# Cross-attention and product-key experts on one core: the experts' first tile begins in four chunks of two heads

## The reference, cut to what matters

```python
x = x + attention(layernorm(x), ctx)
xn = layernorm(x)
q = xn @ w_q                                   # 512 -> 2048 = 16 parts of 128
q = (q - mean(q)) * rsqrt(var(q) + eps) * gamma + beta   # mean, var over all tokens
sim = einsum("pbnhd,hkpd->pbnhk", q, keys)     # 8 heads x 2 sides x 128 scores
sx, ix = top_k(sim[0], 8);  sy, iy = top_k(sim[1], 8)
scores, pk = top_k(sx[:, None] + sy[None, :], 8)         # 8 of 64 sums
indices = ix * 128 + iy at pk                  # 8 heads x 8 = 64 experts a token
h = gelu(x . down_embed[indices]) * softmax(scores)
x = x + sum_k h[k] * up_embed[indices[k]]
```

## Time and profile before

| | us |
|---|---|
| median of 3 runs (lowest to highest) | 3229.04 (3228.68 to 3231.35) |
| the profiled execution, whole | 3229.33 |
| its span in the trace | 3227.2 |
| busy in the span: PE / DVE / ACT / POOL | 2857.5 / 2407.8 / 1820.0 / 2141.3 |
| experts begin (first DVE instruction of the block) | 468.9 |
| first gather issued | 532.85 |
| last gather issued | 3186.17 |

### The profile page before, as it was taken

The page is one execution under the profiler, slowest core; times in us unless marked ns, Lnnn a source line. Parts: engine busy times, 40 slices in busy tenths (PEclk is TensorE's granted clock), DMA queues, the critical chain, the costliest instruction groups (busy, mean ns, idle before and its releaser), DMA issues.

```text
span 3227.2 us, 36087 instructions
## 1 busy us (share of the span) xinstructions
PE 2857.5 (89%) x10310; PEld 1373.1 (43%) x10310; DVE 2407.8 (75%) x5220; ACT 1820.0 (56%) x5589; POOL 2141.3 (66%) x2224
## 2 busy tenths in 40 slices
PE   8999999898888888888888888889888888888877
PEld 6777767343333333333333333333333333333322
DVE  5888715887777777777777777777777777777765
ACT  3566502665565555655656555555656555655554
POOL 1555513777777777777777777777777777777773
PEclk9999999999999999999999999999999999999999
DMA  6222103999999999999999999999999999999996
GB/s 226 80 70 75 39 30 141 395 412 411 413 412 411 412 412 412 411 412 412 412 411 413 412 412 412 412 411 411 412 409 408 411 411 410 411 408 406 409 410 246
DMA packets 324861, 1133.07 MB, mean 351 GB/s; under 512 B 36331, under 2 KB 36971, under 8 KB 324024
## 3 DMA queue, kind: packets, MB, share of 16 engines
q0 software_dynamic: 294912, 1073.87, 83.1%
q1 hardware_dynamic: 29088, 56.41, 4.9%
q10 hardware_dynamic: 664, 0.50, 0.1%
HBM read 1113.87 MB, written 16.78 MB: 350 GB/s over the span
## 4 chain that ended last, share of the span: by engine, by line
DMA 40%; PE 16%; POOL 14%; issue 11%; DVE 4%; ACT 0%; POOLq 0%; ACTq 0%; DVEq 0%
DMA rows<-in_table,expert_idx 37%; POOL rows L785 13%; PE banks L1330 11%; PE banks L1309 3%; DMA expert_more_rows<-in_table,expert_idx 3%; POOL expert_more_rows L785 1%; PE banks L1244 1%; DVE expert_top_i L889 1%; DVE expert_diag L980 1%; DVE rows L966 0%; PE banks L1256 0%; DVE expert_top_s L881 0%; DVE expert_coef L972 0%; PE banks L1285 0%; DVE expert_best_i L912 0%
## 5 line engine op out<-in xcount | busy, mean ns | idle before, releaser
L785 POOL DMA_INDIRECT rows<-in_table,expert_idx x1824 | 1725.1, 946 | 658.0 <-issue 541.0
L1330 PE MATMUL banks<-rows,expert_diag 128*128 128x512 f32 x3648 | 1710.9, 614 | 307.3 <-DVE expert_diag L980 307.0
L1149 ACT ACTIVATE rows<-rows 128x512 f32<-128x512 f32 x1824 | 1124.3, 617 | 945.2 <-DVE expert_coef L972 942.8
L966 DVE TENSOR_TENSOR rows<-rows,banks 128x2048 f32<-128x2048 f32 x456 | 1043.0, 2287 | 543.0 <-DMA rows<-in_table,expert_idx 541.5
L1330 PEld LDWEIGHTS banks<-rows,expert_diag 128*128 128x128 f32 x3648 | 687.4, 194 | 1283.0 <-issue 752.8
L1309 PE MATMUL banks<-amat,expert_xnT 128*128 128x512 f32 x992 | 465.2, 592 | 2.0 <-ACT banks L1140 1.3
L980 DVE TENSOR_TENSOR expert_diag<-banks,expert_coef 128x512 f32<-128x512 f32 x512 | 348.2, 680 | 0.6
L1149 ACT ACTIVATION_READ_ACCUMULATOR rows<-rows 128x1 f32 x1824 | 339.9, 186 | 0.0
L1309 PEld LDWEIGHTS banks<-amat,expert_xnT 128*128 128x128 f32 x992 | 188.3, 190 | 238.8 <-issue 229.9
L785 POOL DMA_INDIRECT expert_more_rows<-in_table,expert_idx x224 | 212.7, 950 | 84.1 <-issue 73.9
L1330 PE MATMUL banks<-expert_more_rows,expert_diag 128*128 128x512 f32 x448 | 209.8, 612 | 39.1 <-DVE expert_diag L980 39.1
(11 more groups left out here) (125 smaller groups left out, 2087.8 us busy)
## 6 DMA issues: line engine op xcount, KB each, us to landing
rows<-in_table,expert_idx POOLq DMA_INDIRECT x1824, 14.6
attention_xT_t<-in_x_T SPq DMA_DIRECT2D x32, 256.0 KB, 3.1
attention_x_t<-in_x SPq DMA_DIRECT2D x32, 256.0 KB, 3.1
x_dram<-rows SPq DMA_DIRECT2D x32, 256.0 KB, 2.0
expert_x_t<-x_dram SPq DMA_DIRECT2D x32, 256.0 KB, 6.1
out_y<-expert_x_t SPq DMA_DIRECT2D x32, 256.0 KB, 6.1
rows<-in_w_q SPq DMA_DIRECT2D x4, 1024.0 KB, 6.1
rows<-in_w_qT SPq DMA_DIRECT2D x4, 1024.0 KB, 8.6
```

Source lines behind the costliest of these rows:

```text
L785: pool.indirect_dma_start(four(n)[:, k, :], None, table[:, :], bass.IndirectOffsetOnAxis(ap=idx[:, t % 2, at:at + 1], axis=0))\
L966: return dve.tensor_tensor(down, down, xn_ps[:, par, :].unsqueeze(1).to_broadcast([P, HALF, D]), ALU.mult)
L1149: ins = act.activation(down, down, ACT.Copy, accum_out=hid[:, j % RING, k:k + 1])
L1330: mm = pe.matmul(out_ps[:, par, :], diag[:, j % RING, k, :], four(t * HALVES + j)[:, k, D:2 * D], start=(j == 0 and k == 0), stop=(j == HA ...
```

## The change

Nothing is different in what is computed, only how and in which order.

1. The query means move forward: the mean-token product is issued after 6 of the last 25 tiles of second moments (before: after 24), ACT keeps it (`mu_kept`), and DVE computes all 16 means and their squares at the end of the attention block (`query_means`).
2. The experts' start is done by quarters. PE interleaves C w for part m, the matrix of a quarter and tile 0's scores from that matrix; `raw_queries`, `norm_queries`, `first_scores` are gone. DVE scales the keys and spreads the offset for a quarter in one instruction each (in `fold`); `keys_scaled` and `offset_wide` lie now in the ring of x2 tiles, so SP's load of tile 2 waits for the matrix.
3. `choose_two(q)` decodes the indices of two heads, and POOL starts the gathers of 4 steps after each of four index events. Chunks 2 and 3 are chosen inside tile 0's steps 1 and 3.
4. Two of POOL's powers stand inside its gather list (ahead of steps 3 and 4); step 4 waits for the last C w, steps 6 and 8 for the matrix.
5. The scores and choices for tile 1 and 2 that stood ahead of the loop are now beside tile 0's steps (`first_tile`, and `beside_first` of ACT and PE). Exponentials of tile 0 are taken for two heads at a time.

```diff
+            def query_means():
+                dve.wait_ge(ev["mu_kept"], 1)
+                dve.wait_ge(w_in, 32 * KC)
+                for m in range(NM):
+                    wait(dve, "mean_done", m - 1)
+                    dve.tensor_tensor_reduce(free[:, m % 2 * D:(m % 2 + 1) * D], mu_row, wq2T[:, m, :],
+                                             1.0, 0.0, ALU.mult, ALU.add, mean_q[:, m:m + 1])\
+                       .then_inc(ev["mean_done"], 1)
...
-            second_moments(len(moments_left) - 1)
+            second_moments(6)
...
-            pe.matmul(out_ps, inv_tokens, xsum, start=True, stop=True)
-            second_moments(1)
+            pe.matmul(out_ps, inv_tokens, xsum, start=True, stop=True).then_inc(ev["mu_done"], 1)
+            second_moments(len(moments_left))
...
+            deviations(0)
+            deviations(1)
             for n in range(NT * HALVES):
                 t, j = divmod(n, HALVES)
-                if j % (HALVES // 2) == 0:
-                    wait(pool, "idx_done", t * 2 + j // (HALVES // 2) + 1)
+                if n in (3, 4):
+                    deviations(n - 1)
+                if t == 0 and j % 4 == 0:
+                    pool.wait_ge(ev["idx_done"], j // 4 + 1)
+                if t > 0 and j % (HALVES // 2) == 0:
+                    pool.wait_ge(ev["idx_done"], NQ + (t - 1) * 2 + j // (HALVES // 2) + 1)
                 if n >= GROUPS:
-                    wait(pool, "up_done", n + 1 - GROUPS)
-                if n == 6:
-                    wait(pool, "amat_done", NM)
+                    pool.wait_ge(ev["up_done"], n + 1 - GROUPS)
+                if n == 4:
+                    pool.wait_ge(ev["yw_done"], NM)
+                if n in (6, 8):
+                    pool.wait_ge(ev["a_done"], NM)
+                    pool.wait_ge(ev["bias_done"], NQ)
...
+            def first_tile():
+                for j in range(HALVES):
+                    dve.wait_ge(row_in[j % GROUPS], (j // GROUPS + 1) * 64)
+                    made_products = products(0, 0, j)
+                    if j == 0:
+                        made_products.then_inc(ev["multiplied"], 1)
+                        fold(NQ - 1)
+                        weigh_two(0)
+                        weigh_two(1)
+                        dve.wait_ge(ev["ident_kept"], 1)
+                    else:
+                        coefficients(0, 0, j - 1)
+                        diagonals(0, j - 1)
+                    if j == 1:
+                        choose_two(2, ())
+                    if j == 3:
+                        choose_two(3, ())
...
+            def beside_first(j):          # PE
+                if j == 8:
+                    turn(2)
+                early = {4: (1, 0), 5: (1, 1), 8: (1, 2), 9: (1, 3), 10: (2, 0), 12: (2, 1), 13: (2, 2),
+                         14: (2, 3)}
+                if j in early:
+                    scores(*early[j])
```

More of the change, by code:

```diff
@@ L715, in ring @@
         return (half % 2) * 2 + par
-    def run(step):
-        for t in range(NT):
-            step(t, t % 2, t // 2, min(3, NT - 1 - t), t == 0)
     with nc.Block() as block:
@@ L989, in finish, with step @@
                 dve.tensor_tensor(x2, out_ps[:, par, :], x2, ALU.add).then_inc(ev["y_done"], 1)
-            def step(t, par, half, more, first):
+            def step(t, par, half, more):
                 for j in range(HALVES):
@@ L994, in step @@
                     dve.wait_ge(row_in[n % GROUPS], (n // GROUPS + 1) * 64)
-                    made_products = products(t, par, j)
-                    if first and j == 0:
-                        made_products.then_inc(ev["multiplied"], 1)
+                    products(t, par, j)
                     if j in (4, 6, 11, 14) and more >= 2:
@@ L1009, in step @@
                             split_places(0)
-                        if not first:
+                        if t > 1:
                             indices(par, 1)
@@ L1023, in step @@
                             keep_marked(0)
-                        if not first:
-                            finish(t - 1, 1 - par, half + par - 1)
+                        finish(t - 1, 1 - par, half + par - 1)
                     if j == 6:
@@ L1069, in step @@
                         diagonals(t, j - 1)
-                    elif not first:
+                    else:
                         diagonals(t - 1, HALVES - 1)
@@ L1104, in _ @@
                 now(pick_marked())
-                indices(0, d)
-            shift_best().then_inc(ev["shifted"], 1)
-            norm(1, 1, 0)
-            wait(dve, "normed", NM)
-            wait(dve, "raw_done", NQ)
-            now(norm_again(0, 0, 0))
-            wait(dve, "exp_done", 1)
-            now(exp_sum())
-            now(exp_inverse())
-            now(weights(0))
-            top(1, 0)
-            top(1, 1)
-            wait(dve, "topped", NQ + 2)
-            now(pair_sums(0))
@@ new lines, in _ @@
+            dve.wait_ge(ev["consts"], 1)
+            now(dve.tensor_copy(iota_f[:, :], iota_u[:, :]))
+            keep_moments(1)
+            keep_moments(2)
+            query_variance(0)
+            norm(0, 0, 0)
+            for m in range(1, 4):
+                query_variance(m)
+            norm_again(0, 0, 0)
+            query_variance(4)
+            fold(0)
+            query_variance(5)
+            query_variance(6)
+            choose_two(0, (7,))
+            query_variance(8)
@@ L1127, in _ @@
+            fold(1)
+            norm(1, 1, 0)
+            query_variance(9)
+            query_variance(10)
+            choose_two(1, (11,))
+            query_variance(12)
+            query_variance(13)
+            fold(2)
+            query_variance(14)
+            query_variance(15)
+            first_tile()
+            for t in range(1, NT):
+                step(t, t % 2, t // 2, min(3, NT - 1 - t))
             coefficients(NT - 1, 1, HALVES - 1)
@@ L1169, in step, with early_seed, exponents_of_two @@
                         turned(t + 3, 1 - par)
-                    if j == 7 and more >= 1:
+                    if t > 0 and j == 7 and more >= 1:
                         exponents()
+            def beside_first(j):
+                if j == 0:
+                    turned(1, 1)
+                if j == 1:
+                    exponents_of_two(2)
+                if j == 3:
+                    exponents_of_two(3)
+                    early_seed(1, 0)
+                if j == 4:
+                    early_seed(1, 1)
+                if j == 6:
+                    early_seed(1, 2)
+                if j == 7:
+                    early_seed(1, 3)
+                if j == 8:
+                    turned(2, 0)
+                if j == 9:
+                    early_seed(2, 0)
+                if j == 10:
+                    early_seed(2, 1)
+                if j == 12:
+                    act.wait_ge(ev["shifted"], NQ + 1)
+                    exponents().then_inc(ev["exp_done"], 1)
+                    early_seed(2, 2)
+                if j == 13:
+                    early_seed(2, 3)
+            def early_seed(t, q):
+                wait(act, "topped", t * NQ + q - 1)
+                seed(q)
+            def exponents_of_two(q):
+                two = slice(2 * q, 2 * q + 2)
+                act.wait_ge(ev["shifted"], q + 1)
+                act.activation(expo[:, two, :], expo[:, two, :], ACT.Exp).then_inc(ev["exp_done"], 1)
             def keep_moments(j):
@@ L1313, in score, with scores, step @@
                     mm.then_inc(ev["scored"], 1)
-            def step(t, par, half, more, first):
+            def scores(t, q):
+                for c in range(KC):
+                    score(t, t % 2, q, c)
+            def step(t, par, half, more):
                 chunk_at = {0: 0, 2: 1, 8: 2, 11: 3}
```

420 lines of the change are left out of this document (227 added, 193 removed).

## The result

| | us | runs |
|---|---|---|
| before | 3229.82 (3228.68 to 3231.61) | 7 |
| after | 3239.47 (3237.34 to 3240.72) | 7 |
| after / before | 1.0028, 95% interval 1.0017 to 1.0040 | |

The changed kernel is slower by 0.28%, some 9.7 us, where I had forecast 3221 and faster. The time lies above my range of 3214.5 to 3228. The profiled execution of after took 3239.55 us (its span 3237.8), 10.2 us more than the one of before.

What follows compares the result with a forecast made beforehand. DMA, full at 411 GB/s, bounds the main loop. From 3229.33 us, 10.7 us of earlier landing off and 2.15 us of clock loss on give 3220.8; 0.29 lower for the median, 3220.5, said as 3221; range 3214.5 to 3228.

Steps and rivals of the forecast that it cites:

- means: Means moved from the experts' variance loop to the attention block: 12 us of DVE, hidden there, so 0 us.
- nothing is won there by itself: Experts' variance loop: PE sets its pace at 2.16 us a part, so removing DVE's mean reductions alone gains nothing.
- the start: Before tile 0's loop: first gather at about 503.4, 29.4 us earlier; DVE at step 1 at 537.1.
- tile 0 gives most of it back: Tile 0's steps: slots wait for updates, DVE leaves at 641.1, 97th gather at 649.3; 10.7 us of advance left.
- the clock takes one loss: Tile 0's early updates: PE's waits lower its granted clock, one loss of 2.15 us on the path.
- The landing that I compare: Landing of the 97th gather (step 24, after tile 0's last update): 655.8 against 666.5, 10.7 us earlier.
- the two waits: PE before tile 0's loop: 2.1 us for scaled keys and 1.5 us for variances, matrix done at about 535.9.
- the 10 us of waits in my sum of 104.0: DVE in tile 0: waits for PE's scores of tiles 1 and 2, which stand behind an update, 10 us.
- tables: ACT's exponential and gelu switches in tile 0: 1.28 us load each on the path, without 1.38 us drain each.
- So the DMA stays full and the 10.7 us are kept to the end.: From tile 1 on: unchanged code, a step of four gathers takes 5.18 us at 411 GB/s, nothing of the advance lost.
- The rivals: Tile 0 takes back more, 0.30; slower, 0.08; advance holds or half, 0.06; start not earlier, 3229 or above.
- the one that ended slower: PE stays at 1.2 GHz until tile 0's step 7: 3248, or about 3233 for half the steps; chance 0.08.

Runs made afterwards that it cites:

- Experiment 11: Changed kernel with more_rows realigned to 512 bytes, and the 16 means and squares back in the experts' variance loop: 3225.07 us, ratio 0.9982 to the kernel before.
- experiment 12: Changed kernel with rows and more_rows at multiples of 512 bytes, PE's scores of tiles 1 and 2 one step earlier: 3164.78 us, 0.9796 to before.
- a_aligned: Changed kernel with 448 unused bytes ahead of more_rows, which then lies at a multiple of 512: 3222.57 us, ratio 0.9975 to the kernel before.
- Experiments 1 to 6: Unused padding tiles: one realigns more_rows in the changed kernel (3222.57 us), five shift more_rows or the tiles behind it in the kernel before (3231.91 to 3250.82 us).
- a_powers_first: a_aligned with all four powers ahead of POOL's gather list and the last fold ahead of the first products: 3229.12 us, ratio 0.9995 to the kernel before.

## Why the prediction was wrong, step by step

**Right: means.** L394 runs from 428.52 and ends by 438.5, inside the second moments; DVE was busy 8.59 us of 430 to 460 us while PE stayed at 30.00. Experiment 11 speaks against my "nothing is won there by itself": back in the variance loop the means cost 2.5 us by the medians and delayed the first gather by 3.1.

**Right: the start.** First gather 503.55 for 503.4, choice 3.25 for 3.45 us, POOL's stand from 525.1 to 528.46 for 525.2 to 529.4, step 1 at 536.52 for 537.1.

**Right in sum, by errors that cancel: tile 0 gives most of it back, and the clock takes one loss.** The 97th gather goes at 651.49; the forecast was 649.3 without and 651.5 with the loss of 2.15 us. Of 29.3 us at the first gather 7.0 are left. PE's updates of after (start us, us, instruction, idle before), which answer to the earlier trace rows and to the updates of the earlier trace rows:

```profile
550.86 8.55 PE L1431 MATMUL banks<-rows,expert_diag 128*128 128x512 f32 x16 [2.78 <-DVE expert_diag L980]
...
563.57 5.40 PE L1431 MATMUL banks<-rows,expert_diag 128*128 128x512 f32 x8 [4.16 <-DVE expert_diag L980]
...
645.29 5.40 PE L1431 MATMUL banks<-rows,expert_diag 128*128 128x512 f32 x8 [3.49 <-DVE expert_diag L980]
```

Three times PE began an update after a wait of 2.78 to 4.16 us, and each time it lost 1.7 to 2.0 us against 3.43 us an update (the first row holds two updates). The granted clock was 0.83 over 550 to 560 us and 0.91 over 640 to 660. I had counted one loss on the path. It fell at the last update of tile 0 too, which I had not counted; but DVE began tile 1's first products at 641.22, where my sum had 641.1 without a loss and 643.3 with the one that I had put on its path. So the end of the tile came out right in part by luck. The landing that I compare came out better than forecast: the 97th gather landed at 655.6 in after and at 666.2 in before, 10.5 us earlier where 10.7 less the clock's 2.15 made 8.5, since it took 4.1 us to land and not the 6.5 that I had assumed. (A slip of the sum: 532.0 and the two waits make 535.6, not 535.9.) That the path goes through PE's scores of tiles 1 and 2 [the 10 us of waits in my sum of 104.0] is borne out by experiment 12: one step earlier, and the 97th gather goes 10.9 us earlier, the clock's losses included.

**Right: tables.** The first coefficients of tile 0 at 541.50 follow the first gelu as summed with the load alone. ACT's timeline of after:

```profile
539.97 1.28 ACT L1269 ACT_TABLE_LOAD   x1
541.26 0.20 ACT L1269 ACTIVATE expert_act_h<-expert_hid 128x4 f32<-128x4 f32 x1
```

The further drain of the Trainium skill ("ScalarE: Activation LUTs", What ACT_TABLE_LOAD costs), which I had left out of the sum, isn't seen: gelu follows the load within 0.01 us.

**Wrong: "So the DMA stays full and the 10.7 us are kept to the end."** It did stay full, at 1.03, but the term before it, the time of a gather (5.18 us for a step of four at 411 GB/s), was taken as unchanged. I wrote "a fixed amount of DMA work" after looking only at instructions and their order. The change part by part should have had one more part: two tiles more in the persistent allocation. It moved the ninth slot group off a 256-byte border, and the pace went from 1.3044 to 1.3136 us a gather at 408 GB/s: 17 us in the trace between the 97th gather and the last. Take these out and the forecast stands: a_aligned measured 3222.57 for 3221, with the errors in tile 0 that cancel. Experiments 1 to 6 show this cause and its border; what the chip does with such a row is not shown beyond the longer packets.

**The rivals.** None of the four was the case, and the one that ended slower had another cause (PE at 1.2 GHz). I gave 0.08 to slower, since I had looked for mechanisms only in the start. I had named the condition on which all of it hangs, that "the main loop's pace is not the same in both" would make it wrong, without asking what could change it.

## What to carry to other kernels

In a loop that is bound by DMA, what a change does to addresses can count as much as what it does to order: after each change of the tiles' list, look at where the buffers of the transfers begin, and put them on a multiple of 256 bytes. Compare GB/s at an equal DMA share; a full queue that moves fewer bytes is a changed price, not a wait. An advance in the start is worth only what is left of it when the last work of the start stops holding up transfers, here 7 of 29 us at the 97th gather; so shorten the path to that release too (12 us in experiment 12, for PE's scores one step earlier), and not only the path to the first transfer. And don't scale a price from a few transfers to all of them: look at the packets' own times first.

## What the runs showed of the hardware that was not expected

- Where the rows of 224 of 2048 gathers into SBUF (128 rows of 4 KB each) began 64 or 128 B past a multiple of 256 and not on one, the program took 17 to 21 us longer, 78 to 92 ns for each of the 224; 256 past a multiple of 512 was free. By the packets' times less than half of that lies in the moved gathers themselves.
- With every row on a border the gain was less than proportional: 1.3044 to 1.2813 us a gather, 411 to 418 GB/s. A row packet of 4096 B then took 159 ns in 99.7% of the cases; with every row off 37% still took 159 ns and nearly all the others 160 to 172, mean 163.4.
- POOL's issue of gathers had a median spacing of 1.24 us where no power stood inside the gather list and 1.25 us where two did, from the 513th gather to the end. While the DMA was the bound it cost nothing: a_aligned and a_powers_first have the same pace, 1.3031 and 1.3040.
